# A graph network's last block computed for the 1561 chosen rows only, with an exact threshold search, row gathers and row scatters

## The reference

```python
x = x + _L1_ffn_ref(_layernorm(x)[None], ...)[0]          # the last line of the reference

weights = (einsum('bsd,do->bso', x, wr) + br)[..., 0]     # here x is the normalized row; s = 3125
k = int(0.5 * s); kk = k - 1                              # 1562 and 1561
_, idx = top_k(weights, k);  sel_idx = idx[:, :kk]
sel = take_along_axis(x, sel_idx)
h = gelu(sel @ w1 + b1)                                   # 256 -> 1024
y = (h @ w2 + b2) * w_sel                                 # 1024 -> 256
return zeros_like(x).at[sel_idx].set(y) + x
```

## Time and profile before

| | us |
|---|---|
| median of 3 runs (1956.3 to 1961.58) | 1959.21 |
| the profiled execution | 1957.89 |
| its span in the trace | 1956.2 |
| mean granted TensorE clock | 0.939 of full speed |
| PE busy | 1741.3 (89%) |
| DVE busy | 1196.0 (61%) |
| ACT busy | 1138.6 (58%) |
| POOL busy | 14.5 (1%) |

### The profile page before, as it was taken

How to read it: one execution, slowest core, us unless ns; L and a number is a source line. 1 busy time by engine, 2 the same in 40 slices (tenths; PEclk the granted TensorE clock), 3 DMA queues, 4 the chain that set the end, 5 groups by cost and what they waited for, 6 DMA issues and landing times. The chain is left out here.

```text
span 1956.2 us, 37752 instructions
## 1 busy us (share of the span) xinstructions
PE 1741.3 (89%) x12416; PEld 1493.9 (76%) x12416; DVE 1196.0 (61%) x1978; ACT 1138.6 (58%) x2061; POOL 14.5 (1%) x35
## 2 busy tenths in 40 slices
PE   5677777699999999959999699999999999969996
PEld 5566666599999999935666599987778887757785
DVE  5598998489999999834444522233222224367997
ACT  1377777688888888723322565655655555533322
POOL 2000000000000000000000000000000000000000
PEclk9878788799999999979999799999999999989998
DMA  7225555253122221010000544445454444521002
GB/s 187 82 64 160 160 147 158 84 129 82 40 68 52 56 68 34 2 30 1 0 0 1 130 113 112 112 117 137 130 129 111 112 112 129 140 63 54 1 1 66
DMA packets 127241, 164.99 MB, mean 84 GB/s; under 512 B 10702, under 2 KB 120533, under 8 KB 127002
## 3 DMA queue, kind: packets, MB, share of 16 engines
q1 hardware_dynamic: 122657, 158.58, 30.1%
q10 hardware_dynamic: 3542, 3.46, 0.8%
q0 software_dynamic: 928, 1.43, 0.3%
HBM read 114.51 MB, written 48.93 MB: 84 GB/s over the span
## 5 line engine op out<-in xcount | busy, mean ns | idle before, releaser
L1525 PE MATMUL ps_sets<-arena,kinds 125*125 125x195 bf16 x2500 | 448.1, 247 | 33.2 <-DVE kinds L1441 32.4
L1405 ACT ACTIVATE kinds<-ed_rows,es_mask 125x625 bf16<-125x625 f32 x500 | 365.7, 809 | 61.8 <-PE ps_sets L1531 30.3
L1531 PE MATMUL ps_sets<-arena,kinds 125*125 125x195 bf16 x2300 | 397.7, 249 | 0.0
L1525 PEld LDWEIGHTS ps_sets<-arena,kinds 125*125 125x125 bf16 x2500 | 343.3, 137 | 40.2 <-DVE kinds L1441 39.8
L2152 ACT ACTIVATE onewide<-onering 125x625 fp32r (+1 forms) x375 | 257.2, 722 | 196.1 <-PE oneps L1945 192.9
L1531 PEld LDWEIGHTS ps_sets<-arena,kinds 125*125 125x125 bf16 x2300 | 309.0, 134 | 0.0
L1945 PE MATMUL oneps<-oneparts_b,onewide 125*125 125x512 f32 x1250 | 294.3, 396 | 0.2 <-DVE onefull L2041 0.2
L1945 PEld LDWEIGHTS oneps<-oneparts_b,onewide 125*125 125x125 f32 x1250 | 231.2, 186 | 61.2 <-DVE onefull L2041 3.3
L1436 DVE TENSOR_TENSOR kinds<-kinds,blk 125x2500 bf16<-125x2500 bf16 x120 | 182.5, 1521 | 36.4 <-ACT kinds L1405 31.2
L779 PE MATMUL ps_hist<-X 128*125 128x125 bf16 x1250 | 127.4, 263 | 57.2 <-DVE X L695 55.3
L1441 DVE TENSOR_TENSOR kinds<-blk,kinds 125x2500 bf16<-125x2500 bf16 (+1 forms) x110 | 167.6, 1523 | 8.2
(11 more groups left out here) (290 smaller groups left out, 2385.1 us busy)
## 6 DMA issues: line engine op xcount, KB each, us to landing
onering<-counts SPq DMA_DIRECT2D x50, 683.6 KB
onering<-countsT SPq DMA_DIRECT2D x50, 683.6 KB
countsT<-tr SPq DMA_DIRECT2D x25, 683.6 KB
blk<-counts SPq DMA_DIRECT2D x20, 546.9 KB
counts<-blk SPq DMA_DIRECT2D x3, 3418.0 KB
counts<-blk_odd SPq DMA_DIRECT2D x2, 3418.0 KB
ed_rows<-ed_dram SPq DMA_DIRECT2D x16, 273.4 KB
onering<-counts SPq DMA_DIRECT2D x50, 79.3 KB
```

The source lines that it names most:

```text
L1405: a.activation(kinds[:, slots(m)[0] + s, 0, :], ed_b[:, h, :], ACT.Relu, scale=MASK_SCALE, bias=k.es_mask[:, t0 + s, h:h + 1]).then_inc(ma ...
L1525: t_.matmul(out[0], kind[0], z[0], start=(t == 0), stop=False)
L1531: last = t_.matmul(out[1], kind[1], z[1], start=False, stop=(t == T - 1))
```

## The change

The last block no longer works on all 25 tiles. It finds the 1561 chosen rows first, gathers them, and runs the two products for 13 tiles (12 of 125 rows and one of 61).

- **During the fourth pass of the convolutions**, now written out in place of a loop: after a batch's `X` is there, ScalarE takes the root for its rows (`roots`), and VectorE computes the router weights (`row_weights`) and the row plus its normalized self (`rest_rows`) into `spare`. GpSimd stores both, the row with its statistics to `x_dram` and the rest to `out`, with five DMAs per batch. `spare` is one buffer, so `rest_rows` waits for the stores of the batch before. This is done for four batches; the fifth is done in the last block.
- **Search**: the threshold, the 1561st largest weight, is found four bits at a time in eight rounds. A round compares 25 weights per partition with 15 candidates (375 elements), sums them, has TensorE add over partitions, and sets four bits.
- **Positions**: running sums over tiles and partitions give each chosen row its place, one-hot tables and 25 small products turn places into row numbers `ids`.
- **Rows**: 13 indirect DMAs on GpSimd gather the rows. Work goes in three groups, of 3, 5 and 5 tiles. Results are scattered to `out` by 13 indirect DMAs, again on GpSimd.

The diff, cut to its core:

```diff
+TOPK = N // 2 - 1
+BITS = 4
+NQ = 2 ** BITS
+NR = 32 // BITS
+XR = F + 4
...
+def row_weights(v, k, std, i, junk):
+
+    tiles = slice(i * U, (i + 1) * U)
+    v.reciprocal(k.stat[:, tiles, 1], std[:, tiles])
+    v.tensor_copy(k.stat[:, tiles, 0], k.MV[:, tiles, 0])
+    v.drain()
+    for u in range(U):
+        t = i * U + u
+        v.scalar_tensor_tensor(out=junk[:, u, :], in0=k.X[:, t, :], scalar=k.stat[:, t, 0:1], in1=k.wr_b[:, :],
+                               op0=ALU.subtract, op1=ALU.mult, accum_out=k.dot[:, t:t + 1])
+    v.drain()
+    v.tensor_tensor(out=k.dot[:, tiles], in0=k.dot[:, tiles], in1=k.stat[:, tiles, 1], op=ALU.mult)
+    v.drain()
+    v.tensor_scalar(k.stat[:, tiles, 2], k.dot[:, tiles], k.br_b[:, 0:1], None, ALU.add)
+    v.drain()
+
+
+def rest_rows(v, k, i, rest):
+
+    for u in range(U):
+        t = i * U + u
+        v.tensor_scalar(rest[:, u, :], k.X[:, t, :], k.stat[:, t, 0:1], k.stat[:, t, 1:2], ALU.subtract, ALU.mult)
+    v.drain()
+    v.tensor_tensor(out=rest[:, :, :], in0=rest[:, :, :], in1=k.X[:, i * U:(i + 1) * U, :], op=ALU.add)
...
+def search_tables(v, k, nib):
+
+    v.tensor_scalar(k.above[:, :], nib, NQ / 2.0, -(2.0 ** 31), ALU.is_ge, ALU.mult)
+    for r in range(NR):
+        v.tensor_scalar(k.step[:, r, :], nib, 32 - BITS * (r + 1), None, ALU.logical_shift_left)
+    v.drain()
+    v.tensor_scalar(k.above[:, :], k.above[:, :], -1.0, None, ALU.add)
+    v.drain()
+    v.tensor_copy(k.above_i[:, :], k.above[:, :])
+    v.drain()
+    v.tensor_tensor(out=k.step[:, 0, :], in0=k.step[:, 0, :], in1=k.above_i[:, :], op=ALU.bitwise_xor)
...
+                for i in range(U - 1):
+                    tiles = slice(i * U, (i + 1) * U)
+                    pool.wait_ge(rest_done, i + 1)
+                    for lo_, hi_ in SPLIT:
+                        pool.dma_start(rows_of_block(k.x_dram, i)[lo_:hi_, :, 0:F], X[lo_:hi_, tiles, :]).then_inc(rest_stored, 16)
+                        pool.dma_start(rows_of_block(k.out, i)[lo_:hi_], spare[lo_:hi_]).then_inc(rest_stored, 16)
+                    pool.dma_start(rows_of_block(k.x_dram, i)[:, :, F:XR], k.stat[:, tiles, :]).then_inc(rest_stored, 16)
+                pool.wait_ge(rest_stored, 80 * (U - 1))
...
+                dve.wait_ge(ints_done, 1)
+                search_tables(v, k, tab_i[:, T + 1:T + NQ])
+                v.memset(k.stat[:, :, 3:4], 0.0)
+                dve.wait_ge(router_in, 32)
+
+                def rest(i):
+                    dve.wait_ge(root_done, i + 1)
+                    row_weights(v, k, std, i, raw[:, :, 0:F])
+                    if i:
+                        dve.wait_ge(rest_stored, 80 * i)
+                    rest_rows(v, k, i, spare)
+                    v.nop().then_inc(rest_done, 1)
...
-                for n in range(4):
+                for n in range(3):
...
+                dve.wait_ge(hi_done, 4 * U)
+                for i in range(U):
+                    if i == U - 1:
+                        rest(i - 1)
+                    means_out(3, i)
+                    rows_out(3, i)
+                    v.nop().then_inc(x_done, 1)
+                    if 0 < i < U - 1:
+                        rest(i - 1)
...
+                def roots(i):
+                    act.wait_ge(x_done, i + 1)
+                    a.activation(std[:, i * U:(i + 1) * U], k.MV[:, i * U:(i + 1) * U, 1], ACT.Sqrt, bias=eps[:, 0:1])
+                    a.drain().then_inc(root_done, 1)
...
+                for i in range(1, U):
+                    widen(3, i, {3 * U + 4: lambda: roots(i - 1)})
...
-    I1 = 2 * HB8
-    TOPK = N // 2 - 1
+    NT = (TOPK + P - 1) // P
+    TAIL = TOPK - (NT - 1) * P
+    GROUP = ((0, 3), (3, 5), (8, NT - 8))
+    NGR = len(GROUP)
+    ROWS = [P] * (NT - 1) + [TAIL]
...
+                pool.wait_ge(ids_done, 1)
+                pool.wait_ge(x_stored, 48)
+                for g, (t0, n) in enumerate(GROUP):
+                    for c in range(t0, t0 + n):
+                        m = ROWS[c]
+                        g_.indirect_dma_start(out=xg[0:m, c, :], out_offset=None, in_=k.x_dram,
+                                              in_offset=bass.IndirectOffsetOnAxis(ap=ids[0:m, c:c + 1], axis=0)).then_inc(rows_in[g], 16)
+                pool.wait_ge(rest_stored, 32)
+                for c in range(NT):
+                    m = ROWS[c]
+                    pool.wait_ge(y_done, c + 1)
+                    g_.indirect_dma_start(out=k.out, out_offset=bass.IndirectOffsetOnAxis(ap=ids[0:m, c:c + 1], axis=0),
+                                          in_=xg[0:m, c, 0:F], in_offset=None).then_inc(y_stored, 16)
...
-                    for t in range(i * U, (i + 1) * U):
-                        c = t * P
-                        if t:
-                            v.tensor_scalar(junk[:, 0:c], w_row[:, 0:c], wt[:, t:t + 1], 0.0, ALU.is_ge, ALU.add, accum_out=ge[:, t:t + 1])
-                            v.drain()
-                        v.tensor_scalar(junk[:, c:N], w_row[:, c:N], wt[:, t:t + 1], 0.0, ALU.is_gt, ALU.add, accum_out=gt[:, t:t + 1])
-                        v.drain()
-                        v.scalar_tensor_tensor(out=junk[:, c:c + P], in0=w_row[:, c:c + P], scalar=wt[:, t:t + 1], in1=before[:, :],
-                                               op0=ALU.is_equal, op1=ALU.mult, accum_out=tie[:, t:t + 1])
...
+                row_weights(v, k, std, L, junk)
+                v.tensor_copy(wcol[:, :], k.stat[:, :, 2])
+                v.drain().then_inc(wt_done, 1)
+                for r in range(NR):
+                    low = 32 - BITS * (r + 1)
+                    if r:
+                        v.tensor_tensor(out=bits[:, :], in0=k.step[:, r, :], in1=now[:, :].to_broadcast([P, NQ - 1]), op=ALU.bitwise_xor)
+                        v.drain()
+                    levels = (bits[:, :] if r else k.step[:, 0, :]).bitcast(FP32)
+                    v.tensor_tensor(out=ge[:, :, :], in0=wcol[:, :].unsqueeze(1).to_broadcast([P, NQ - 1, T]),
+                                    in1=levels.unsqueeze(2).to_broadcast([P, NQ - 1, T]), op=ALU.is_ge)
+                    v.drain()
+                    v.tensor_reduce(out=cnt[:, :], in_=ge[:, :, :], axis=AXX, op=ALU.add)
+                    v.drain().then_inc(cnt_done, 1)
+                    dve.wait_ge(sum_psum, r + 1)
+                    v.tensor_scalar(ind[:, :], ps_o[0:P, 0, r * NQ:r * NQ + NQ - 1], float(TOPK), 0.0, ALU.is_ge, ALU.add,
+                                    accum_out=found[:, r:r + 1])
...
+                        v.tensor_scalar(sel_i[:, :], found[:, r:r + 1], float(2 ** low), None, ALU.mult)
+                    v.drain()
+                    v.tensor_tensor(out=now[:, :], in0=now[:, :], in1=sel_i[:, :], op=ALU.bitwise_xor)
...
+                v.tensor_scalar(mask[:, 0, :], wcol[:, :], tau, None, ALU.is_gt)
+                v.tensor_scalar(mask[:, 1, :], wcol[:, :], tau, None, ALU.is_equal)
+                v.drain().then_inc(mask_done, 1)
+                dve.wait_ge(mask_psum, 1)
+                both = ps_o[0:P, 2, 0:4 * T].rearrange("p (j e t) -> p j e t", j=2, e=2)
+                v.tensor_copy(run[:, 0, :, SCAN:], both[:, 1, :, :])
+                v.drain()
+                for n, d in enumerate((1, 2, 4, 8, 16)):
+                    v.tensor_tensor(out=run[:, (n + 1) % 2, :, SCAN:], in0=run[:, n % 2, :, SCAN:],
+                                    in1=run[:, n % 2, :, SCAN - d:SCAN - d + T], op=ALU.add)
...
+                v.scalar_tensor_tensor(out=lo[:, :], in0=hi[:, :], scalar=-float(P), in1=pos[:, :], op0=ALU.mult, op1=ALU.add)
+                v.tensor_tensor(out=hot_hi[:, :, :], in0=k.tile_no[:, 0:NT].unsqueeze(1).to_broadcast([P, T, NT]),
+                                in1=hi[:, :].unsqueeze(2).to_broadcast([P, T, NT]), op=ALU.is_equal)
+                v.drain()
+                v.tensor_tensor(out=hot_lo[:, :, :], in0=k.iota_row[0:P, :].unsqueeze(1).to_broadcast([P, T, P]),
+                                in1=lo[:, :].unsqueeze(2).to_broadcast([P, T, P]), op=ALU.is_equal)
+                v.tensor_tensor(out=ids2[:, :, 0, :], in0=hot_hi[:, :, :], in1=k.tile_no[:, 0:T].unsqueeze(2).to_broadcast([P, T, NT]), op=ALU.mult)
+                v.tensor_scalar(ids2[:, :, 1, :], hot_hi[:, :, :], k.lane_f[:, 0:1], None, ALU.mult)
...
+                rest_rows(v, k, L, rest)
+                v.nop().then_inc(rest_done, 1)
+                def normalize(g):
+                    t0, n = GROUP[g]
+                    dve.wait_ge(rows_in[g], 16 * n)
...
+                for r in range(NR):
+                    pe.wait_ge(cnt_done, r + 1)
+                    t_.matmul(ps_o[0:P, 0, r * NQ:r * NQ + NQ - 1], k.ones[0:P, 0:P], cnt[:, :], start=True, stop=True).then_inc(sum_psum, 1)
+                pe.wait_ge(mask_done, 1)
+                t_.matmul(ps_o[0:P, 2, 0:2 * T], k.earlier[:, :], mask[:, :, :].rearrange("p e t -> p (e t)"), start=True, stop=True)
```

(16 more changed lines are left out.)

376 lines of the change are left out of this document (219 added, 157 removed).

## The result

The changed kernel takes **1922.5 us** (median of 4 runs, 1921.7 to 1925.0) against 1957.8 for the kernel before in the same job: 0.982, with an interval of 0.980 to 0.984. The profiled execution took 1922.98, its span is 1921.2. The forecast was 1922, and 1921.0 for the profiled execution, 2 us short of what it took. Nearly as close is the last block as a whole: it opens at 1764.5 and is over at 1921.2, 156.7 us, where the sum said 156.0. Several of its terms were not that good, and their errors cancelled.

What follows compares the result with a forecast made beforehand. TensorE and VectorE, both full in the last block, were taken as the bound. Its terms sum to 156.0 us against 199.2, 43.2 saved; less 6.3 lost in the convolutions, 36.9, giving 1922 us, range 1906 to 1942.

Steps and rivals of the forecast that it cites:

- TensorE's terms: Last block, three groups from first transposes to last results: 95.8 us, bounds 93 and 100.
- The clock at the start: First hidden layer of the last block: granted clock 0.50 after TensorE's idle time, 2.8 us lost.
- The convolutions: Fourth pass: `rest_rows` of the fourth batch waits for the third set's stores; 6.3 us lost, bounds 0.1 and 11.
- The opening of the convolutions: Start of the convolutions: tables hidden in VectorE's idle time; two more loads cost 0 to 1 us, taken at 0.
- The search: Last block: eight rounds of 3.3 us, with the first round's extras 26.7 us, bounds 22 and 36.
- First rows: Last block, from the ids: three gathers issued and landed before TensorE starts, 7.1 us, bounds 5.5 and 12.
- The end: Last block: final addition and product, then 6.2 us as for the present store; 7.4 us, bounds 5.5 and 11.
- Rival 1: End of the last block: the 61-row scatter moves on few DMA engines, 2 us more, 1924 us; chance 0.20.
- Rival 2: Search: serial chain costs more, at 5.5 us a round 1940 us; chance 0.10 up to 1945, 0.04 beyond.
- rival 3: Chain costs less: stores land at once, rounds of 2.8 us, fast one-hot table; 1910 us, chance 0.12.
- rival 4: Last block: GpSimd's 26 row transfers become the bound; at 6 us each 1972 us, slower; chance 0.04.
- rival 5: Last block: groups padded to five tiles, so TensorE does 15 of 25 tiles, not 13; no chance set aside.

Runs made afterwards that it cites:

- h_bits_2: Changed kernel with the search in 16 rounds of 2 bits in place of 8 rounds of 4: 1939.1 us, 0.989.
- i_rows_twice: Changed kernel with the same rows gathered once more, unread, ahead of each of the 13 gathers and 13 scatters: 1933.1 us, 0.988.
- k_all_together: Changed kernel with row stores first and counted apart, router loads/tables and `f_rest` store later, 61-row tile ending group two, 32 idle products: 1908.4 us.
- a_same: The changed kernel measured once more, unchanged, as yardstick for the other runs: 1926.0 us, 0.984 of the kernel before.
- d_small_tile_early: Changed kernel with the 61-row tile worked third instead of last: 1923.2 us, 0.983 of the kernel before.
- j_warm_38: Changed kernel with 38 unused fp32 products on TensorE while it waits for the first rows: 1921.6 us, 0.982.

## Why the prediction was right

**The frame held.** TensorE's halved work, with a search, positions and a gather in front of it and nothing hidden, was the right picture: the block is 156.7 us against 156.0, and `h_bits_2` shows that the front really lies on the path, while `i_rows_twice` shows that the row transfers do not, save at the ends. TensorE's terms came from rows of the same instructions and are right to 1 us; the second and third hidden layer took 17.0 and 15.3 for 17 and 15.2. The clock at the start cost less than its 2.8 us: against `k_all_together`, where it stayed at 1.00, the first transposes and hidden layer took 2.0 us longer in the changed kernel and 2.6 in `a_same`.

**The total is luck.** By the table the misses are 7.4 us one way and 5.5 the other, and its first row hides two more: a loss in the last pass that was 1.2 us smaller than forecast, and some 3 us at the opening of the convolutions that were not forecast.

**The convolutions.** The stores' wait has the right size for the wrong reason. Forecast: the batch ends 6.3 us late, with the last store counted 5 us after the last issue, 4 of them for 16-byte pieces. Measured: from the fourth batch's statistics to the fifth's 34.4 us against 29.3 (34.1 in `a_same`), so 4.8 to 5.1 lost. Most of it is the bytes and the issue of both row stores: taking the pieces out of the count made the wait 0.75 us shorter, issuing the awaited store first as well 4.4. The sum had the bytes at nothing; it should have divided 1.28 MB by the pace that the engines reach. Its price for the issue of 560 rows, 1.2 us by a slope from two other loads, was too high as well: 0.81.

**The opening of the convolutions** is the step that failed: "The two more loads there: 0 to 1, taken at 0", and the tables under cover. Together they cost some 3 us, above the upper bound. The prediction had looked at VectorE's idle time there, which covers the tables' use, and not at ScalarE's wait for the ring, which was already the last to end. The execution before opened 0.3 later and had 1.0 more in its passes, and the gap at the block's start grew 0.7, so that the block opened 7.5 us late.

**The search** was over-priced, 3.3 a round for 2.86. The large operations were about right (0.62 from the comparison's start to the sum's, and 0.54 for the sum, for 0.63 each). The handovers were mis-sized: from the sum's end to the result in VectorE 0.72 us, for about 0.9, and the four small operations take 0.98, for 1.14. Eight times 0.44 is 3.5 us; the first round's further small instructions took 1.0, for 0.3. The 25 bf16 products took 2.8, for 3.7; the one-hot table 3.42, for 3.3.

**First rows**: 9.2 for 7.1. Issue of three gathers was right (1.5 apart, the first 0.13 us longer beside VectorE's five subtractions, against 0.3 forecast). Landing was not: 4.5 us for 2.2, and 1.5 of the 2.3 is the store of `f_rest` that SyncE starts into them; the other 0.8 is open. The prediction counted that VectorE's part of the fifth batch meets the gathers, but not its store. The Trainium skill, "SBUF — State Buffer" (the trap that DVE blocks DMA), allowed up to 1.7 us for GpSimd being shut out beside those subtractions, if it lasted for all five. The trace has 0.13 us on GpSimd, and one of the five subtractions at 0.69 us where the others took 0.40 to 0.41.

**The end**: 11.5 for 7.4. Rival 1 is what happened, and its price was right in size (2 us; taking the tile away from the end gives 2.6). The other 1.5 is in the 8.8 us of `d_small_tile_early`, where a tile of 125 rows is last: 1.0 of VectorE, 0.6 until GpSimd is through with the tiles ahead, 1.2 of issue, 2.4 until its rows have moved, and 3.6 without traffic. The prediction had carried over the 6.2 us of a plain store whole.

**The rivals.** Rival 2 (5.5 a round) is out with 2.86; rival 3 came halfway, in the rounds; rival 4 is out by `i_rows_twice`; rival 5 did not occur, the last group has 61 rows.

## What to carry to other kernels

When work on a path is replaced by a serial chain, price every round from rows of small instructions and one handover; the sum comes out within a few us, but the seams (a store beside the first gather, two loads ahead of a ring, the last transfer) decide the rest. A buffer's release is worth the bytes that stand ahead of it on its DMA queue: issue the store that somebody waits for first, and give it its own count. Put a tile whose rows leave on few DMA engines (here the one of 61) where other work hides its transfer, in the middle.

## What was not expected of the hardware

- An indirect transfer of 61 rows of 1 KB takes GpSimd 1.68 to 1.72 us to issue, and one of 125 rows 1.2: fewer rows, longer, and then it moves in some 4 us at a DMA share of 0.07, one engine of 16.
- A plain store of 625 pieces of 16 bytes takes GpSimd 1.66 us to issue, and 560 rows of 1 KB 0.81.
- The granted clock fell from 1.00 to 0.50 while TensorE was in its first hidden layer, after 1.1 and 0.5 us of idle time around the transposes; with idle products running right up to the rows it stayed at 1.00. Why the first case falls is open: the runs tell only that filling most of a gap did not hold the clock (`j_warm_38`), and filling all of it did (`k_all_together`).
